# Key projection of the fourth head pair in an attention schedule: round 3 in place of round 5, and the last residual load behind round 5's transfers

## The chip, the core and the metric

The kernel runs on one core of a Trainium2 chip. A core has five engines that follow their own instruction lists and meet at semaphores: TensorE (PE, with its weight loads as PEld), VectorE (DVE), ScalarE (ACT), GpSimd (POOL) and SyncE (SP), which here issues all DMA transfers. The metric is the device time of one execution in microseconds.

## What is computed

Eight batches of 512 x 512 go through a gated cross attention and then through a gated mixture-of-experts self attention. The change touches the second part only:

```python
def _L0_ffn_ref(x, Wq, Wk, Ws, Wd, Wv, Wo):
    q = (x @ Wq).reshape(b, t, h, dh).transpose(0, 2, 1, 3)
    k = (x @ Wk).reshape(b, t, h, dh).transpose(0, 2, 1, 3)
    gl_v = (x @ Ws).reshape(b, t, h, e)
    wv = _topk_mask(gl_v, SEL) * jax.nn.sigmoid(gl_v)
    xv = jnp.einsum('btd,edk->btek', x, Wv)
    v = jnp.einsum('bthe,btek->bhtk', wv, xv)
    scores = jnp.einsum('bhid,bhjd->bhij', q * scale, k)
    probs = jax.nn.softmax(scores, axis=-1)
    attn = jnp.einsum('bhij,bhjd->bihd', probs, v)
    mask_o = _topk_mask(x @ Wd, SEL)
    return jnp.einsum('bthe,bthk,ekd->btd', mask_o, attn, Wo)

x = x + jnp.tanh(g_ffn[0]) * _L0_ffn_ref(_layernorm(x, axis=-1), ...)
```

There are 8 heads of 64 (4 pairs), 5 experts, 2 of them selected, 512 tokens and a model width of 512 per batch.

## The kernel before

The first part of the program (up to about 488 us of the profile) is the cross attention, which is not touched. The second, `expert_attention`, treats a batch in rounds. A batch has 32 tiles of scores (8 heads by 4 row tiles of 128 x 512), and a round is four of them, one for each of four PSUM banks: rounds 0 to 7 make the scores, pair p of heads using rounds 2p and 2p+1. Everything else of the batch is a unit that hangs at a round and at one of five places in it: SCORES, BEFORE, TURNS, BEHIND, AFTER. The table `AT` (line 1216 on) says where: `turn_y` transposes the normalised input, `experts` makes the expert values and logits, `q` and `k` project the queries and keys of a pair, `values` multiplies probabilities and mixed values, `turn_o` transposes a pair's output, `turn_z` and `result` make the output projection. Within a place, units come in the order in which the table was filled, so queries come ahead of keys.

Consecutive batches overlap. The loop `Fori(0, B - 1)` runs rounds 5 to 12 of batch b, and at each of their places also rounds -3 to 4 of batch b+1 (`CUT = 5`). So round 5 is joined with -3, round 7 with -1, round 8 with 0, round 11 with 3 and round 12 with 4. Ahead of the loop stand rounds -3 to 4 of the first batch, under a table `FIRST_AT` made from `AT` with four exceptions; behind it stand round 5 of the last batch by the same table and then `last_rounds`, written out by hand.

A projection is twelve matmuls of 128 x 512 (line 2219; `wk` is the keys' weight, the queries' lies in `c_t`). Each value is kept as a rounded part and a remainder: ScalarE copies the rounded part out of PSUM (`part_hi`, line 1735, keys at 1761) and VectorE subtracts it for the low part (`part_lo`, line 1928, keys at 1942). The units share three PSUM banks in ring order (`RING = 3`, `bank_of`): a unit's matmuls wait until the unit three places ahead in `ORDER` has been read (`wait_bank`, line 2180).

On the other engines the same tables set the order. VectorE takes row maxima (line 1880), transposes blocks of probabilities (1886), and makes the products of pair outputs and coefficients (1900). ScalarE exponentiates (1701), copies transposed probabilities (1710), normalises the next input (1679, in round -3) and copies expert tiles (1751, 1754). Before the first copy of a batch's expert tiles it waits until GpSimd has mixed all four pairs of the batch before. GpSimd mixes the experts' values of a pair (`mix_values`, lines 1610 and 1616) and adds products (1628). In rounds 4, 6 and 7 (`ALL_BY_VECTOR`) VectorE transposes all tiles in blocks; in the others TensorE transposes half of them (line 2281) and the rest goes through VectorE and DMA.

SyncE moves the block-transposed probabilities into place (`move_blocks`, line 1533: four DMAs of 128 KB for each half), loads the next input, stores the four output tiles of a batch, waits until they have landed and loads the next residual into the buffer that they came from. The values of pair p wait for the moves of rounds 2p and 2p+1.

Of the kernel before, what the change touches and what calls it, by code (L numbers as in the profile page):

```python
# [1167 lines left out]
def expert_attention(nc, block, both, x1, g_ffn, wk, wo, out):  # L1168
# [3 lines left out]
    B, T, D = x1.shape  # L1172
# [32 lines left out]
    SCORES, BEFORE, TURNS, BEHIND, AFTER = range(5)  # L1205
# [10 lines left out]
    AT = {}  # L1216
# [4 lines left out]
        AT["result", t] = ((12, BEFORE), (12, BEFORE), (12, BEHIND), (12, BEHIND))[t]  # L1221
    for p in range(PAIRS):
        AT["q", p] = ((-1, BEFORE), (0, BEHIND), (2, BEFORE), (3, BEFORE))[p]
        AT["k", p] = ((-1, BEFORE), (1, BEFORE), (2, BEHIND), (5, BEFORE))[p]
        AT["values", p] = ((3, AFTER), (5, AFTER), (7, BEHIND), (9, BEHIND))[p]
        AT["turn_o", p] = ((5, BEFORE), (7, BEFORE), (9, BEFORE), (10, BEFORE))[p]
    for k in range(KZ):
# [44 lines left out]
    with ExitStack() as mem:  # L1272
# [130 lines left out]
        def of(dram, b):  # L1403
            return dram[bass.ds(b, 1)].rearrange("o p t d -> (o p) t d")
# [16 lines left out]
        def blocks(r, i):  # L1421

            if i:
                return probs_odd[r % 2].rearrange("p s t -> p (s t)").rearrange("p (j s a) -> p j s a", s=2, a=BLOCK)
            return probs_even[:, r % 2]
# [25 lines left out]
        def by_rows(place):  # L1451

            return pt[:, place].rearrange("p k t -> p (k t)").rearrange("p (r q k s a) -> p r q k s a", r=2, q=QUADS,
                                                                        k=NT, s=2)
# [4 lines left out]
        def passing(name, half, k):  # L1459
            return raw[name][own_rows(name, half, k), k, :]  # L1460
# [4 lines left out]
        def first_end(eng):  # L1465

            eng.wait_ge(both.feat_ps, B * NT)
            eng.wait_ge(both.x1_ready, B * NT)
# [20 lines left out]
        def heads_moved(r):  # L1489
            return range(2 if r in ALL_BY_VECTOR else 1)  # L1490

        def tiles_moved(r):

            return sum(2 * len(heads_moved(i)) for i in range(r))
# [25 lines left out]
        @block.sync  # L1520
        def _(sp):
            def load_x1(b):
                sp.dma_start(stage[:], of(x1_dram, b)).then_inc(x1_loaded, 16)

            def load_residual(b):
                sp.dma_start(x_res[:], of(x1_dram, b)).then_inc(xres_loaded, 16)

            def store(b):
                for t in range(NT):
                    sp.wait_ge(out_ready, NT + b * NT + t + 1)  # L1530
                    sp.dma_start(of(out_dram, b)[:, t, :], x_res[:, t, :]).then_inc(out_stored, 16)

            def move_blocks(b, r, first=False):

                p = r // 2
                for i in heads_moved(r):
                    sp.wait_ge(blocks_turned, b * tiles_moved(ROUNDS) + tiles_moved(r) + 2 * i + 2)
                    if first and p == 2 and i == 0:

                        sp.wait_ge(o_ps, p - 1)  # L1540
                    for q in range(QUADS):
                        sp.dma_start(by_rows((2 * p + i) % 4)[:, r % 2, q].rearrange("p k s a -> p (k s a)"),
                                     blocks(r, i)[q * BLOCK:(q + 1) * BLOCK].rearrange(
                                         "p (j k) s a -> p j (k s a)", j=QUADS)).then_inc(moved[r % 2], 16)

            def steady(b, more):
                for r in range(CUT, ROUNDS):
                    move_blocks(b, r)
                    if more and r == CUT + 1:

                        sp.wait_ge(yt_ps, b * NT + 2 * NT)
                        load_x1(b + 2)
                for r in range(CUT):
                    move_blocks(b + 1, r)
                store(b)

                sp.wait_ge(out_stored, (b + 1) * NT * 16)
                load_residual(b + 1)

            first_end(sp)  # L1560
            for k in range(LAST):
                sp.dma_start(passing("wo", 0, k), wo[k * P:(k + 1) * P, :]).then_inc(wo_loaded[k], 16)
            for place in (0, HALF):
                sp.dma_start(wo_raw[place:place + HALF, LAST, :], wo[LAST * P:NV, :]).then_inc(wo_loaded[LAST], 16)
            sp.dma_start(gate_raw[:], g_ffn.partition_broadcast(P)).then_inc(gate_loaded, 16)

            sp.wait_ge(both.x1_stored, B * NT * 16)
            sp.wait_ge(both.x1_stats_done, B * NT)
            load_residual(0)

            sp.wait_ge(yt_ps, NT)
            load_x1(1)
            for r in range(CUT):
                move_blocks(0, r, True)
            with sp.Fori(0, B - 2) as b:
                steady(b, True)
            steady(B - 2, False)
            move_blocks(B - 1, CUT)
            for t in range(NT - 1):
                sp.wait_ge(out_ready, NT + (B - 1) * NT + t + 1)  # L1580
                sp.dma_start(of(out_dram, B - 1)[:, t, :], x_res[:, t, :]).then_inc(out_stored, 16)
            for half, cols in enumerate(LAST_COLS):
                sp.wait_ge(out_ready, NT + B * NT + half)
                sp.dma_start(of(out_dram, B - 1)[:, NT - 1, cols], x_res[:, NT - 1, cols]).then_inc(out_stored, 16)
            sp.wait_ge(out_stored, (B * NT + 1) * 16)
# [832 lines left out]
def program(nc, x, ctx, ctx_t, g_xattn, g_ffn, w_sim, w_sim_cols, b_sim, w_qv, b_qv, wq, wk, w_vsd, wo, x1, out):  # L2418
    B, T, D = x.shape
    NT, ND = T // P, D // P  # L2420
    with ExitStack() as mem:
        def sb(name, shape, dt=F32):
            return mem.enter_context(nc.sbuf_tensor(name, shape, dt))

        def sem(name):
            return mem.enter_context(nc.semaphore(name))


        x1_norm, x1_stats = sb("x1_norm", [P, 2, B * NT]), sb("x1_stats", [P, NT, 6])
        sb("fill", [P, 8])  # L2430
        both = Both(
            x1_norm=x1_norm, x1_stats=x1_stats, ident=sb("ident", [P, P]),
            x_sb=sb("x_sb", [P, NT, D]), stage=sb("stage", [P, NT, D]), spare=sb("spare", [P, 2, ND, D]),
            tmp=sb("tmp", [P, ND, T]), c_t2=sb("c_t2", [P, 2, ND, T], F32R), c_2=sb("c_2", [P, 2, NT, D], F32R),
            es_t2=sb("es_t2", [P, 2, ND, T], F32R), feat_ps=sem("feat_ps"), hc_ready=sem("hc_ready"),
            et_lo=sem("et_lo"), xb_ready=sem("xb_ready"),
            x1_ready=sem("x1_ready"), x1_stored=sem("x1_stored"), x1_stats_done=sem("x1_stats_done"),
            wx_loaded=sem("wx_loaded"), wq_loaded=sem("wq_loaded"), wk_loaded=sem("wk_loaded"), wx_hi=sem("wx_hi"),
            wx_lo=sem("wx_lo"), wq_hi=sem("wq_hi"), wq_lo=sem("wq_lo"), y_act=sem("y_act"), yt_ps=sem("yt_ps"),
            yt_hi=sem("yt_hi"), yt_lo=sem("yt_lo"))  # L2440
        block = mem.enter_context(nc.Block())
        cross_attention(nc, block, both, x, ctx, ctx_t, g_xattn, w_sim, w_sim_cols, b_sim, w_qv, b_qv, x1, w_vsd, wq, wk)
        expert_attention(nc, block, both, x1, g_ffn, wk, wo, out)
# [43 lines left out]
```

## Time and profile before

| | |
|---|---|
| time, median of 3 runs | 1133.11 us (1133.0 to 1133.26) |
| the profiled execution | 1133.13 us, of it span 1131.2 us |
| busy in the span: PE | 1100.8 us (97%) |
| busy: PEld | 836.7 us (74%) |
| busy: DVE | 925.1 us (82%) |
| busy: ACT | 567.4 us (50%) |
| busy: POOL | 657.4 us (58%) |
| granted TensorE clock over the span | 0.998 |

Times in the profile are microseconds from the start of the span. The busy shares are averages over both parts of the program. A row of a timeline names the start, the duration, the engine, the line of the kernel, what is written and read, how many instructions were merged into it (x12), and in brackets how long the engine was idle before it and what ended that. The ends of matmuls are modelled, so the distance between two starts says more of TensorE than a duration does.

### The profile page before, as it was taken

How to read it: one execution, taken by the hardware profiler on the slowest of the kernel's cores; microseconds unless marked ns; L12 is line 12 of the kernel's file. 1: busy time of each engine (PE TensorE's matmuls, PEld its weight loads, DVE VectorE, ACT ScalarE, POOL GpSimd, SP SyncE). 2: the span in 40 equal slices, each digit the busy share in tenths (PEclk: the TensorE clock that was granted, in tenths of full speed). 3: DMA queues.
4: the chain of work that ended last, by engine and by line, in shares of the span. 5: the costliest groups of instructions: out<-in, count | busy, mean ns of one | idle time of the engine just before them, and what ended most of it. 6: DMA issues, size and time to landing. Idle time of an engine off the chain costs nothing.

```text
span 1131.2 us, 18705 instructions
## 1 busy us (share of the span) xinstructions
PE 1100.8 (97%) x5709; PEld 836.7 (74%) x5709; DVE 925.1 (82%) x1609; ACT 567.4 (50%) x1295; POOL 657.4 (58%) x476
## 2 busy tenths in 40 slices
PE   7999999999999999999899999999999999999988
PEld 6888888888888888886666666767667666767656
DVE  7988787878777785758798897898988988978986
ACT  7644444344434343446655555455556545555533
POOL 2645252524333342337949759579499498596794
PEclk9999999999999999999999999999999999999999
DMA  5441414141414132442423524524426335244241
GB/s 205 149 140 47 131 56 130 56 130 56 130 56 130 56 93 72 144 132 69 127 75 93 171 71 124 154 56 137 123 56 190 88 74 178 77 115 128 52 137 38
DMA packets 89277, 119.97 MB, mean 106 GB/s; under 512 B 9120, under 2 KB 52896, under 8 KB 89248
## 3 DMA queue, kind: packets, MB, share of 16 engines
q1 hardware_dynamic: 89248, 119.61, 35.5%
q8 instruction: 15, 0.25, 0.1%
q14 instruction: 14, 0.11, 0.0%
HBM read 58.76 MB, written 16.78 MB: 67 GB/s over the span
## 4 chain that ended last, share of the span: by engine, by line
PE 70%; POOL 13%; DVE 9%; issue 5%; ACT 2%; DMA 0%; POOLq 0%; DVEq 0%; ACTq 0%
PE ps_f L992 23%; PE ps_s L992 8%; PE ps_o L2297 7%; PE ps_h L992 7%; POOL spare L1610 7%; PE ps_r L2219 6%; POOL spare L1616 5%; PE ps_r L2252 5%; PE ps_s L2273 5%; PE ps_r L2228 4%; DVE nmax L1880 2%; DVE beaten L1969 1%; POOL z L1628 1%; PE ps_r L2210 1%; DVE z_tmp L1900 1%
## 5 line engine op out<-in xcount | busy, mean ns | idle before, releaser
L1610 POOL TENSOR_TENSOR spare<-xv,pick 128x512 f32<-128x512 f32 x160 | 184.9, 1156 | 35.2 <-DVE pick L1996 22.3
L1880 DVE TENSOR_REDUCE nmax<-ps_s 128x1 f32<-128x512 f32 x256 | 158.2, 679 | 48.4 <-PE ps_s L2273 47.4
L1616 POOL TENSOR_TENSOR spare<-spare 128x512 f32<-128x512 f32 x128 | 165.8, 1295 | 10.0
L1628 POOL TENSOR_TENSOR z<-z,z_tmp 128x1280 f32<-128x1280 f32 x35 | 102.7, 2933 | 117.2 <-DVE z_tmp L1900 114.8
L1701 ACT ACTIVATE tmp<-ps_s,nmax 128x512 f32<-128x512 f32 x124 | 86.1, 695 | 106.8 <-DVE nmax L1880 106.8
L2297 PE MATMUL ps_o<-pt,spare 128*64 128x512 f32 x496 | 114.8, 605 | 9.4 <-POOL spare L1616 5.1
L254 POOL TENSOR_TENSOR e_t<-e_t 128x512 fp32r<-128x512 f32 x28 | 35.4, 1298 | 135.4 <-ACT e_t L510 135.4
L2273 PE MATMUL ps_s<-k,q 64*128 64x512 f32 x768 | 106.4, 408 | 0.7 <-ACT pt L1710 0.7
L2273 PEld LDWEIGHTS ps_s<-k,q 64*128 64x128 f32 x768 | 67.3, 184 | 42.9 <-issue 29.8
L254 POOL TENSOR_TENSOR c<-stage,c 128x512 fp32r<-128x512 f32 x28 | 41.3, 1508 | 95.9 <-ACT c L250 95.8
L2219 PE MATMUL ps_r<-es_t,c_t 128*128 128x512 f32 x384 | 96.2, 399 | 0.0
L2219 PE MATMUL ps_r<-es_t,wk 128*128 128x512 f32 x384 | 95.1, 396 | 0.0
L992 PE MATMUL ps_s<-c_t,es_t 128*128 128x512 f32 x384 | 92.5, 393 | 2.6 <-DVE es_t L727 2.6
L992 PE MATMUL ps_f<-wec,e_t 128*128 128x512 f32 x384 | 92.1, 392 | 0.0
L992 PE MATMUL ps_f<-weh,eh_t 128*128 128x512 f32 x384 | 91.9, 391 | 0.0
L992 PE MATMUL ps_f<-wh,h_t 128*128 128x512 f32 x384 | 91.3, 389 | 0.5 <-DVE h_t L887 0.5
L992 PE MATMUL ps_h<-es_t,c 128*128 128x512 f32 x384 | 88.7, 390 | 0.2 <-DVE es_t L781 0.2
L2297 PEld LDWEIGHTS ps_o<-pt,spare 128*64 128x64 f32 x496 | 33.4, 138 | 70.8 <-issue 64.0
L992 PEld LDWEIGHTS ps_s<-c_t,es_t 128*128 128x128 f32 x384 | 71.1, 188 | 17.8 <-DVE es_t L727 3.1
L992 PEld LDWEIGHTS ps_f<-wh,h_t 128*128 128x128 f32 x384 | 72.0, 188 | 15.9 <-DVE h_t L887 0.9
L992 PEld LDWEIGHTS ps_h<-es_t,c 128*128 128x128 f32 x384 | 71.9, 188 | 15.1 <-DVE es_t L781 0.3
L1886 DVE STREAM_TRANSPOSE tmp<-tmp 128x1024 f32<-128x1024 f32 x62 | 76.6, 1236 | 7.6 <-ACT tmp L1701 7.6
(253 smaller groups left out, 2272.4 us busy)
## 6 DMA issues: line engine op xcount, KB each, us to landing
pt<-tmp SPq DMA_DIRECT2D x248, 128.0 KB, 2.6
stage<-in_x SPq DMA_DIRECT2D x32, 256.0 KB, 3.3
x_sb<-in_x SPq DMA_DIRECT2D x8, 1024.0 KB, 5.2
x_dram<-x_sb SPq DMA_DIRECT2D x32, 256.0 KB, 3.1
stage<-x_dram SPq DMA_DIRECT2D x8, 1024.0 KB, 5.5
x_sb<-x_dram SPq DMA_DIRECT2D x8, 1024.0 KB, 5.7
out_dram<-x_sb SPq DMA_DIRECT2D x31, 256.0 KB, 2.7
pt<-probs_odd SPq DMA_DIRECT2D x60, 128.0 KB, 2.7
```

Of the source, the lines that this page charges most:

```text
L254: return eng.tensor_tensor(pair[:, 1, k, :], operand[:, k, :], pair[:, 0, k, :].bitcast(F32), ALU.subtract)
L992: last = pe.matmul(out, left(l, k), right(r, k), start=start and n == 1, stop=stop and n == ND * len(PASSES))
L1610: pool.tensor_tensor(v_tmp[:] if e else acc, xv[:, :, e, :].unsqueeze(2).broadcast_to(shape), pick[:, e, :, 2 * p:2 * p + 2].unsqueeze(3). ...
L1616: pool.tensor_tensor(acc, acc, v_tmp[:], ALU.add).then_inc(v_steps, 1)
L1628: pool.tensor_tensor(zv, zv, z_tmp[:, h % 2], ALU.add).then_inc(z_pool, 1)
L1701: act.activation(out, scores, ACT.Exp, bias=nmax[:, n:n + 1], accum_out=den[:, h, t:t + 1]).then_inc(p_exp, 1)
L1880: dve.tensor_reduce(nmax[:, n:n + 1], ps_s[:, n % BANKS, :], AX_X, ALU.max, negate=True).then_inc(nmax_ready, 1)
L1886: dve.transpose(both_tiles, both_tiles).then_inc(blocks_turned, 2)
L2219: end = pe.matmul(ps, w2[:, l, k, n * P:(n + 1) * P], y_t2[:, r, k, :], start=m == 0, stop=m == len(every) - 1)
L2252: end = pe.matmul(ps, z_t2[:, zt(l, k), n * P:(n + 1) * P], wo2[:, r, k, :], start=m == 0, stop=m == len(every) - 1)
L2273: end = pe.matmul(ps_s[:, (n + a) % BANKS, :], q2[head_rows(a), p % 2, l, t * P:(t + 1) * P], k2[head_rows(a), p % 2, r, :], start=m == 0, ...
L2297: end = pe.matmul(ps_o[head_rows(a), :], v_acc[:, p, k, a, :], rows, start=k == 0, stop=k == NT - 1)
```

## The change

The fourth pair's keys (pairs are counted from 0, so k3) are projected in round 3, behind the same pair's queries, and no longer in round 5. `FIRST_AT` takes the entry over, so this holds for the first batch too. On SyncE, in the run-down of the loop, the wait for the stored output of the last batch but one and the load of the last batch's residual now stand behind the moves of round 5 of the last batch; in the other turns the order is as it was.

```diff
@@
-        AT["k", p] = ((-1, BEFORE), (1, BEFORE), (2, BEHIND), (5, BEFORE))[p]
+        AT["k", p] = ((-1, BEFORE), (1, BEFORE), (2, BEHIND), (3, BEFORE))[p]
@@
                 for r in range(CUT):
                     move_blocks(b + 1, r)
                 store(b)
+                if more:
+                    replace_result(b)
+
+            def replace_result(b):
 
                 sp.wait_ge(out_stored, (b + 1) * NT * 16)
                 load_residual(b + 1)
@@
             steady(B - 2, False)
+
             move_blocks(B - 1, CUT)
+            replace_result(B - 2)
```

The lines behind the edit move by 4 to 6: the projections' matmuls are at 2225 after the change, the scores' at 2279.

On TensorE, at the joined round 11 and 3, before the change: q3 (`c_t`), then two tiles of probabilities (2281), the z transposes (2242) and the values of pair 0 (2297).

```order
L2219 MATMUL ps_r<-es_t,c_t 128x512 x12
L2279 REGISTER_ALU
L2281 MATMUL ps_s<-ident,spare 128x128 x4
L2279 REGISTER_ALU
L2281 MATMUL ps_s<-ident,spare 128x128 x4
L2238 REGISTER_ALU
L2242 MATMUL ps_r<-ident,z 128x128 x12
```

The same place after the change:

```order
L2225 MATMUL ps_r<-es_t,c_t 128x512 x12
L2225 MATMUL ps_r<-es_t,wk 128x512 x12
L2285 REGISTER_ALU
L2287 MATMUL ps_s<-ident,spare 128x128 x4
L2285 REGISTER_ALU
L2287 MATMUL ps_s<-ident,spare 128x128 x4
L2244 REGISTER_ALU
L2248 MATMUL ps_r<-ident,z 128x128 x12
```

Twelve key matmuls (`wk`) now stand between the queries' and the transposes.

On TensorE, at the joined round 5 and -3 of the loop, before the change: turn_o of pair 0 (2234), k3 (2219), two tiles of probabilities and the first of the four turn_y (2210).

```order
L2234 MATMUL ps_r<-ident,spare 128x128 x4
L2178 REGISTER_ALU
L2213 REGISTER_ALU
L2219 MATMUL ps_r<-es_t,wk 128x512 x12
L2279 REGISTER_ALU
L2281 MATMUL ps_s<-ident,spare 128x128 x4
L2279 REGISTER_ALU
L2281 MATMUL ps_s<-ident,spare 128x128 x4
L2178 REGISTER_ALU
L2208 ISA
L2210 MATMUL ps_r<-ident,stage 128x128 x4
```

The same place after the change:

```order
L2240 MATMUL ps_r<-ident,spare 128x128 x4
L2285 REGISTER_ALU
L2287 MATMUL ps_s<-ident,spare 128x128 x4
L2285 REGISTER_ALU
L2287 MATMUL ps_s<-ident,spare 128x128 x4
L2184 REGISTER_ALU
L2214 ISA
L2216 MATMUL ps_r<-ident,stage 128x128 x4
```

Only transposes are left there between the scores and the values of pair 1.

On SyncE, behind the loop, before the change: the stores of the last batch but one, the residual and the moves of round 5 of the last batch.

```order
L1542 DMA pt<-probs_odd 128x1x256 x4
L1531 DMA out_dram<-x_sb 128x512 x4
L1526 DMA x_sb<-x_dram 128x4x512
L1542 DMA pt<-tmp 128x1x256 x4
L1581 DMA out_dram<-x_sb 128x512 x3
```

The same place after the change:

```order
L1542 DMA pt<-probs_odd 128x1x256 x4
L1531 DMA out_dram<-x_sb 128x512 x4
L1542 DMA pt<-tmp 128x1x256 x4
L1526 DMA x_sb<-x_dram 128x4x512
L1587 DMA out_dram<-x_sb 128x512 x3
```

The moves and the residual have changed places.

## Rows read from the trace of the kernel before

**Rows 1.** The page, part 4: the chain that ended last, share by engine.

```profile
PE 70%; POOL 13%; DVE 9%; issue 5%; ACT 2%; DMA 0%; POOLq 0%; DVEq 0%; ACTq 0%
```

**Rows 2.** TensorE's waits: waiting line, releaser, us in total, times, longest.

```profile
PE ps_o L2297 <- POOL spare L1616: 5.1, 7, 0.7
```

**Rows 3.** Timeline of TensorE, joined rounds 11 and 3: q3 to the values.

```profile
752.57 3.03 PE L2219 MATMUL ps_r<-es_t,c_t 128*128 128x512 f32 x12
755.43 0.60 PE L2281 MATMUL ps_s<-ident,spare 128*128 128x128 f32 x4
...
757.09 1.53 PE L2242 MATMUL ps_r<-ident,z 128*128 128x128 f32 x12 [0.24 <-DVE z L1911]
759.36 3.65 PE L2297 MATMUL ps_o<-pt,spare 128*64 128x512 f32 x16 [0.73 <-POOL spare L1616]
```

**Rows 4.** Timelines of TensorE and ScalarE at round 7.

```profile
713.76 1.66 PE L2273 MATMUL ps_s<-k,q 64*128 64x512 f32 x12
...
714.68 0.24 ACT L1751 ACTIVATE logits<-ps_r 128x80 f32<-128x80 f32 x1 [4.04 <-POOL spare L1616]
...
715.35 0.66 PE L2234 MATMUL ps_r<-ident,spare 128*128 128x128 f32 x4
```

**Rows 5.** Timeline of TensorE in round 5, one weight load (PEld) with its wait.

```profile
693.88 1.66 PE L2273 MATMUL ps_s<-k,q 64*128 64x512 f32 x12
...
695.88 3.01 PE L2219 MATMUL ps_r<-es_t,wk 128*128 128x512 f32 x12
698.73 1.03 PE L2281 MATMUL ps_s<-ident,spare 128*128 128x128 f32 x8
699.60 1.34 PE L2210 MATMUL ps_r<-ident,stage 128*128 128x128 f32 x8
...
700.28 0.42 PEld L2210 LDWEIGHTS ps_r<-ident,stage 128*128 128x128 f32 x4 [0.32 <-ACT stage L1679]
...
700.87 3.65 PE L2297 MATMUL ps_o<-pt,spare 128*64 128x512 f32 x16
```

**Rows 6.** Timeline of ScalarE in round 5: first exponential, second normalised tile.

```profile
695.69 0.69 ACT L1701 ACTIVATE tmp<-ps_s,nmax 128x512 f32<-128x512 f32 x1 [6.29 <-DVE nmax L1880]
...
699.39 0.80 ACT L1679 ACTIVATE stage<-stage,norm 128x512 f32<-128x512 f32 x1
```

**Rows 7.** Timeline of TensorE, round 7 of the loop's first turn.

```profile
559.11 0.63 PE L2234 MATMUL ps_r<-ident,spare 128*128 128x128 f32 x4 [2.28 <-ACT logits L1751]
```

**Rows 8.** Timeline of TensorE in the last batch.

```profile
1095.50 0.66 PE L2234 MATMUL ps_r<-ident,spare 128*128 128x128 f32 x4
1100.39 5.22 PE L2297 MATMUL ps_o<-pt,spare 128*64 128x512 f32 x16 [4.23 <-issue]
...
1109.83 1.95 PE L2324 MATMUL ps_o<-pt,spare 128*64 128x256 f32 x16
```

**Rows 9.** Timeline of VectorE in round 5 of the last batch.

```profile
1090.70 0.68 DVE L1942 TENSOR_TENSOR k<-ps_r,k 128x512 fp32r<-128x512 f32 x1
...
1091.48 1.23 DVE L1886 STREAM_TRANSPOSE tmp<-tmp 128x1024 f32<-128x1024 f32 x1
```

**Rows 10.** SyncE's moves of round 5; landing of L1542 from 1092, and 1060 to 1090.

```profile
1093.38 2.77 SPq L1542 DMA_DIRECT2D pt<-tmp  x4
...
DMA to landing us min/median/max: 4.6/5.1/5.5
...
DMA to landing us min/median/max: 2.5/2.6/2.9
```

**Rows 11.** Timeline of GpSimd: the first sum behind its mixing.

```profile
1107.45 2.94 POOL L1642 TENSOR_TENSOR z<-z,z_tmp 128x1280 f32<-128x1280 f32 x1
```

**Rows 12.** Stretches: us, busy by engine, then granted clock, DMA share, GB/s.

```profile
1100.40:1105.60 5.20, 5.20 (x17) 1.61 (x18) 2.25 (x1) 0.00 (x0) 4.96 (x4) 0.69 0.01 3
```

**Rows 13.** Timeline of TensorE at the start of the kernel.

```profile
4.43 3.84 PE L999 MATMUL ps_b<-ident 128*128 128x128 f32 x18 [4.43 <-DVE stats L663]
...
9.44 1.04 PE L999 MATMUL ps_b<-ident 128*128 128x128 f32 x8
```

## The prediction

> **What bounds the kernel now.** I read the chain that ended last first, then TensorE's waits, then the timeline of one turn of the attention loop on each engine, then the end of the program. The chain is mostly TensorE, with a share of GpSimd [rows 1]: TensorE works nearly without a gap, so what counts is where its few gaps lie and who ends them. The reader should find two places.
>
> The first is round 11 of batch b, which is also round 3 of batch b+1. The projection of q3 starts at 752.57, the values of pair 0 start at 759.36 [rows 3], 6.79 us later. What runs in between is 2.86 for q3 (752.57 to 755.43), 0.87 for eight transposes of probabilities (698.73 to 699.60 [rows 5]) and 1.31 for the twelve transposes of z at the same pace, 5.04 in all. So 1.75 us are gaps: 0.73 of idle that GpSimd's mixing of the values ends and 0.24 that z ends, the rest lying in the modelled ends of matmuls. The wait for GpSimd comes seven times, once in each turn [rows 2].
>
> The second is round 7. There turn_o of pair 1 starts at 715.35. TensorE was ready just then (the scores start at 713.76 and hold it for 1.59), and so was the bank: ScalarE copied the first expert tile from 714.68 on, once GpSimd had mixed the last pair of the batch before [rows 4]. Two cycles are thus equally long, TensorE's own work with its gaps and GpSimd's mixing with the way back over turn_o, the scores, VectorE's products and the sums. A turn takes 78.12 us by either: from 559.11 in the first turn [rows 7] to 715.35 two turns later. This says at once that the loop can't gain: less work on TensorE would meet GpSimd at round 7. It can lose, if TensorE's own cycle grows.
>
> **Moving k3 in the loop.** The twelve matmuls cost 2.85 (695.88 to 698.73 [rows 5]).
> Added in round 3: between q3 and the values of pair 0 TensorE now has 5.04 + 2.85 = 7.89 us of work where it has 6.79 with its gaps. All gaps are covered, GpSimd is ready at 759.3 and the values start at about 760.45: 1.10 us later. ScalarE gets k3's copy ahead of its probability copies, VectorE the low part ahead of its block transpose. The last z transpose now goes to the bank that k3 used. VectorE's low part takes 0.68 [rows 9] and ScalarE's copy about as much, so that bank is free some 1.4 behind the end of k3; TensorE asks for it behind eight transposes and two thirds of the z transposes, 0.87 + 0.88 = 1.75. I take 0 for it, and 0.3 a turn as its bound.
> Removed in round 5: here the question is what stands behind k3. After the scores (693.88) VectorE takes the row maxima, ScalarE exponentiates from 695.69, then normalises two tiles of the next input, the second from 699.39 on; TensorE's weight load for the second turn_y waits for exactly that tile (idle 0.32, ended by ScalarE) and begins at 700.28, and the values of pair 1 follow at 700.87 [rows 5, 6]. That chain of 6.99 us from the scores to the values holds no k3: its copy on ScalarE comes behind both tiles, and its low part on VectorE comes behind the maxima. TensorE today fills that stretch with k3 and is just in time. With k3 gone it idles up to 2.85 us in small pieces and starts the values 6.99 after the scores as before. I take 0 for the gain; the bounds are 0 and 2.85, and the row with the wait for ScalarE stands for 0.
> So TensorE's cycle grows by 1.10 - 0 and GpSimd's no longer ties. From turn_o of round 7 in the first turn to the same place in the last there are six full turns: 6 x 1.10 = 6.6 us.
>
> **Before the loop and in its first turn.** The table for the first batch takes the new place too, so 2.85 are added in its round 3. Its round 5 is the first of the loop, with the same chain, and gives nothing back. But in that turn TensorE waits 2.28 at turn_o for GpSimd, which mixes from the first pick without a stop and is not touched [rows 7]. Cover 2.28, so 2.85 - 2.28 = 0.57 at most, 0 at least if some of the later gaps absorb it. I take 0.3.
>
> **The last batch.** Its rounds 3 and 4 are in the last turn and come 1.10 late against turn_o of that turn, as above. Then two edits meet. TensorE's turn_o of pair 1 is issued at 1095.50 and the values of pair 2 start only at 1100.39, after 4.23 of idle that no engine ended [rows 8]: they wait for the transfers of round 5. These four were issued from 1093.38 on, right behind a residual load of 1 MB, and took 4.6 to 5.5 us to land, where those of the rounds before took 2.5 to 2.9 [rows 10]. Now they go ahead of it. The blocks that they carry are transposed at 1091.48, behind the low part of k3 (some 0.6 of VectorE's time) [rows 9]; without that and with 1.10 of delay they are ready 0.5 later. The issues then start near 1093.2, the last one near 1095.2, and it lands by 1098.1. The values of pair 2 start 2.3 earlier. TensorE's idle before them shrinks from 4.23 to some 1.6, and with it may go the low clock: the granted clock was 0.69 from 1100.40 to 1105.60 and those 16 matmuls took 5.22 [rows 8, 12], against 3.65 in the loop. That is 1.57 more, 3.9 in all.
> What is late next is GpSimd. The first half of the last pair's values starts at 1109.83 [rows 8], and the mixing that it reads ended as GpSimd's first sum started, at 1107.45 [rows 11]. GpSimd's times hang on the last turn's round 8 and not on k3. So the end of the kernel can follow the values by 1109.83 - 1107.45 = 2.4 us and no more; the sums behind it, on GpSimd too, give the same. I take -2.35, with bounds of -1.2 (the transfers land late) and -3.6 (one collision less between VectorE's sums and GpSimd's mixing).
> The residual itself is read some 25 us after its new issue: nothing.
>
> **The sum.** The profiled execution took 1133.13 with a span of 1131.2 (the median of the runs is 1133.11): 1133.13 + 0.3 + 6.6 - 2.35 = 1137.7 us, 0.40% slower.
>
> **A rule against the rows.** At the start of the kernel TensorE runs transposes alone: eighteen from 4.43 take 3.84, 0.21 each, and eight from 9.44 take 1.04, 0.13 each [rows 13]. So transposes alone brought the fast pace. The Trainium skill, page "TensorE: Matmul & The Clock Gate", section "Part 4: PE-mode transpose", says that transposes don't count as work for the clock. By that rule the emptied round 5, where only transposes are left between the scores and the values, would fall to the lower clock. By it the sum is that of the clock's rival below, 1149; by the first rows of this kernel it stays at 1137.7, and I go by the rows.
>
> **Rivals.**
> *The stretch in round 5 does shrink.* If what makes the second turn_y late is partly k3 (a queue, a port), the values of pair 1 come earlier. From 1.10 on, the loss of round 3 is paid back and GpSimd binds at turn_o again: a turn takes 78.12, and the sum is 1133.13 + 0.3 - 2.35 = 1131.1, with the end's bound 1129.8. Against it: the weight load's wait names ScalarE's tile [rows 5]. Chance 0.13, half of it beyond 0.2%.
> *Half of it.* Part of the gaps in round 3 survive beside k3, or some 0.5 comes back in round 5: 0.3 to 0.6 a turn, 1133 to 1135. Chance 0.16.
> *The clock falls in round 5.* Between scores and values TensorE would idle for most of 5.4 us, which the tail's row prices: 1.57 more for sixteen value matmuls, in seven turns 11 us, so 1149. For it: after 4.23 of idle the clock was low [rows 12]. Against it: after the 2.28 of idle in the first turn turn_o took 0.63, as the 0.66 elsewhere [rows 4, 7], the pieces of idle here are shorter than that, and transposes stand between them [rows 13]. Chance 0.05.
> *The added matmuls are not added.* Each batch still projects k3 once, so the work is the same; a reader might expect no change. This sum, 1133.1 less whatever the end gives, holds only where TensorE alone binds at both places; it doesn't [rows 4, 5]. It would end with the first rival and has its chance there.
>
> **How the numbers follow.** The forecast has 0.66, with 1135.8 to 1140 for itself: the end's bounds give +1.2 and -1.2, the bank of k3 up to +2, the first turn 0.3 each way. This kernel's runs can tell 0.2% (2.3 us) from no change, so the same is 1130.9 to 1135.4. Faster: half the first rival, 0.07. Same: the other half and most of the second, 0.20. Slower: forecast, clock and the rest, 0.73. The range of 1132.5 to 1140 leaves out the first rival and the clock, 0.18.
>
> **What would show it.** Starts of turn_o in round 7 lie 79.2 apart, not 78.12. No wait for GpSimd at the values of pair 0, but several short ones for ScalarE in round 5, with 6.99 us from scores to values. The idle before the last batch's values of pair 2 under 2 us, with their sixteen matmuls back at 3.6, and a new wait for GpSimd's mixing before the last pair's. The forecast is wrong if the values of pair 1 follow the scores by less than 6.9, or if turns stay at 78.1.

## The result and the profile of the kernel after

| | before | after |
|---|---|---|
| median | 1133.11 us (1133.0 to 1135.09, 5 runs) | 1140.74 us (1140.43 to 1143.86, 5 runs) |
| after : before | | 1.007, interval 1.0055 to 1.0085 |
| profiled execution, span | 1133.13 us, 1131.2 us | 1143.86 us, 1142.1 us |
| granted clock over the span | 0.998 | 0.991 (0.994 in the other four) |

The change makes the kernel 0.7% slower. The direction was forecast; the time, 1137.7, was not, and 1140.74 lies above the range. The profiled execution of after is its longest, so where a size is given below it is that of this execution, and the medians of the experiments stand beside it. The ratios here and below compare the runs of both kernels as a whole, so they are not exactly the ratios of the medians beside them.

The page's chain, by engine, of after. GpSimd, which had 13% before [rows 1], is no longer in it:

```profile
PE 90%; ACT 5%; DVE 3%; issue 2%; DMA 0%; ACTq 0%; DVEq 0%
```

TensorE's waits in after (line, releaser, us in total, times, longest):

```profile
PE ps_s L2287 <- ACT spare L1707: 14.8, 16, 2.0
...
PE ps_o L2303 <- issue: 2.0, 1, 2.0
PE ps_r L2216 <- ACT stage L1685: 1.7, 5, 0.4
```

The seven waits for GpSimd at the values [rows 2] are gone. In their place stand sixteen for ScalarE's exponentials, two in each of the eight rounds 5, which the keys have left.

**Round 3**, TensorE's timeline (start, duration, operation), to be held against [rows 3]:

```profile
758.15 3.02 PE L2225 MATMUL ps_r<-es_t,c_t 128*128 128x512 f32 x12
761.01 2.89 PE L2225 MATMUL ps_r<-es_t,wk 128*128 128x512 f32 x12
763.74 1.03 PE L2287 MATMUL ps_s<-ident,spare 128*128 128x128 f32 x8
764.61 1.47 PE L2248 MATMUL ps_r<-ident,z 128*128 128x128 f32 x12
766.02 3.65 PE L2303 MATMUL ps_o<-pt,spare 128*64 128x512 f32 x16
```

From the start of q3 to the start of the values it is now 7.87 us, 1.08 more than before, with no idle left.

**Round 5, a turn at full clock**, to be held against [rows 5]:

```profile
699.57 1.66 PE L2279 MATMUL ps_s<-k,q 64*128 64x512 f32 x12
701.16 0.66 PE L2240 MATMUL ps_r<-ident,spare 128*128 128x128 f32 x4
702.87 0.66 PE L2287 MATMUL ps_s<-ident,spare 128*128 128x128 f32 x4 [1.06 <-ACT spare L1707]
704.21 0.66 PE L2287 MATMUL ps_s<-ident,spare 128*128 128x128 f32 x4 [0.68 <-ACT spare L1707]
705.21 1.36 PE L2216 MATMUL ps_r<-ident,stage 128*128 128x128 f32 x8 [0.35 <-ACT stage L1685]
706.51 3.65 PE L2303 MATMUL ps_o<-pt,spare 128*64 128x512 f32 x16
```

The values follow the scores after 6.94 us, nearly as before (6.99). The 2.85 us of keys have become 2.09 us of idle in three pieces, all ended by ScalarE; the rest lies in ends that are modelled. Only 0.05 is given back.

**Round 5, one turn later:**

```profile
784.34 1.82 PE L2216 MATMUL ps_r<-ident,stage 128*128 128x128 f32 x8 [0.35 <-ACT stage L1685]
786.09 4.63 PE L2303 MATMUL ps_o<-pt,spare 128*64 128x512 f32 x16
```

The idle is the same, but turn_y takes 1.82 instead of 1.36 and the values 4.63 instead of 3.65. The stretches show why (us, busy by engine, granted clock, DMA share, GB/s):

```profile
702.00:706.00 4.00, 2.04 (x13) 1.33 (x14) 4.00 (x5) 3.91 (x12) 3.77 (x4) 1.00 0.92 257
781.00:786.00 5.00, 2.97 (x16) 1.99 (x16) 5.00 (x6) 4.91 (x14) 4.69 (x5) 0.87 0.92 289
786.00:791.00 5.00, 5.00 (x20) 1.69 (x20) 2.33 (x3) 2.32 (x4) 4.69 (x5) 0.79 0.52 161
1023.00:1028.00 5.00, 4.86 (x18) 2.19 (x20) 4.14 (x5) 4.08 (x8) 4.69 (x5) 0.66 0.66 188
```

The column behind the five engines is the granted clock. It went from 2.4 to 1.2 GHz for part of the stretch: the mean is 0.87 and 0.79 in this turn and 0.66 in the round 5 at 1023, but 1.00 at 702.

**The turns.** A turn is measured from turn_o of round 7 to the next one. Here is one in which the clock fell:

```profile
720.97 0.66 PE L2240 MATMUL ps_r<-ident,spare 128*128 128x128 f32 x4
...
801.54 0.65 PE L2240 MATMUL ps_r<-ident,spare 128*128 128x128 f32 x4
```

turn_o of round 7 starts at 561.94, 641.88, 720.97, 801.54, 880.65, 959.75 and 1040.39. The six distances are 79.94, 79.09, 80.57, 79.11, 79.10 and 80.64, where before had six of 78.10 to 78.15, 78.12 in the mean. So there are two kinds of turn: three of about 79.10, and three that are 0.84, 1.47 and 1.54 longer, the ones in which the clock fell in round 5. It fell also in the round 5 ahead of the first of these starts, where the first piece of idle was 2.03 us long and the values took 5.29:

```profile
541.60 0.66 PE L2287 MATMUL ps_s<-ident,spare 128*128 128x128 f32 x4 [2.03 <-ACT spare L1707]
...
545.84 5.29 PE L2303 MATMUL ps_o<-pt,spare 128*64 128x512 f32 x16
```

**The last batch**, to be held against [rows 8]; first TensorE, then SyncE's issues, then GpSimd:

```profile
1108.40 0.66 PE L2240 MATMUL ps_r<-ident,spare 128*128 128x128 f32 x4
1111.05 5.35 PE L2303 MATMUL ps_o<-pt,spare 128*64 128x512 f32 x16 [1.99 <-issue]
...
1120.62 1.95 PE L2330 MATMUL ps_o<-pt,spare 128*64 128x256 f32 x16
```

```profile
1106.37 2.51 SPq L1542 DMA_DIRECT2D pt<-tmp  x4
1108.92 0.61 SPq L1526 DMA_DIRECT2D x_sb<-x_dram  x1
```

```profile
1119.86 2.91 POOL L1648 TENSOR_TENSOR z<-z,z_tmp 128x1280 f32<-128x1280 f32 x1
```

The moves now go ahead of the residual and land in 2.5 to 2.7 us (4.6 to 5.5 before [rows 10]). The idle before the values of pair 2 shrank from 4.23 to 1.99. But the sixteen matmuls behind it still took 5.35.

**The account** of the profiled executions: +2.83 up to the first turn_o, +9.72 in six turns (6 x 0.98 = 5.9 of it at full clock, 3.85 by the clock), -1.7 from the last turn_o to the end (101.7 instead of 103.4). That is 10.85, and the spans differ by 10.9.

### The profile page after: what moved, and what is told of

Read it like the earlier page. It is cut to its first block, busy times and chain, and to the rows that moved or that the text cites. A ratio compares the mean times of both kernels' runs of the same rounds, so it can differ in the third digit from the quotient of the medians.

```text
span 1142.1 us, 18712 instructions
## 1 busy us (share of the span) xinstructions
PE 1109.3 (97%) x5709; PEld 841.3 (74%) x5709; DVE 931.0 (82%) x1609; ACT 568.3 (50%) x1295; POOL 658.0 (58%) x476
## 4 chain that ended last, share of the span: by engine, by line
PE 90%; ACT 5%; DVE 3%; issue 2%; DMA 0%; ACTq 0%; DVEq 0%
PE ps_f L992 23%; PE ps_r L2225 15%; PE ps_o L2303 10%; PE ps_s L992 8%; PE ps_s L2279 8%; PE ps_h L992 7%; PE ps_r L2258 5%; PE ps_r L2234 4%; PE ps_s L2287 3%; PE ps_r L2216 1%; ACT tmp L1707 1%; PE ps_r L2240 1%; DVE nmax L1886 1%; ACT probs_odd L1707 1%; ACT spare L1707 1%
## 5 line engine op out<-in xcount | busy, mean ns | idle before, releaser
L2303 PE MATMUL ps_o<-pt,spare 128*64 128x512 f32 x496 | 118.9, 623 | 2.0 <-issue 2.0
```

The lines of the kernel that those rows point to most:

```text
L2303: end = pe.matmul(ps_o[head_rows(a), :], v_acc[:, p, k, a, :], rows, start=k == 0, stop=k == NT - 1)
```

## Experiments

Theory: three things add up. TensorE's turn grows by about 1 us since its cycle no longer ties with GpSimd's; the residual's new place gains 1 to 2 us; and TensorE's clock falls in some of the emptied rounds 5. Rivals: the excess lies in the residual's new place; it lies in something that the keys bring to round 3; the 2.85 us come back in round 5 and are lost elsewhere. Runs of one group were measured beside the same runs of the kernel before, whose median was 1135.02 in the first group (keys_only to fill_transposes), 1135.22 in the second (more_in_round_3 to tail_fill_only), 1133.75 in the third and 1135.13 for the last kernel. The ratios are to those runs. The kernel before has executions near 1133.3 and near 1135.1 (see the last experiment), and how many of each a group holds moves its ratios by about 0.1%. So 1.007 of the kernel after, whose five runs of before were nearly all of the short kind, and the ratios of the experiments are compared below by the kernels' own medians too.

### The two halves of the change

```diff
-        AT["k", p] = ((-1, BEFORE), (1, BEFORE), (2, BEHIND), (5, BEFORE))[p]
+        AT["k", p] = ((-1, BEFORE), (1, BEFORE), (2, BEHIND), (3, BEFORE))[p]
```

> Only the keys of pair 3 move to round 3; the last residual is loaded where it was. Theory (a turn grows by 1.0 to 1.1 us since round 3 gains more work than it had gaps and round 5 gives nothing back; in the emptied round 5 the clock falls in some turns, 0.9 to 1.5 us each; the end gains 1.7 by the residual): the loop as in the changed kernel, turns of 79.1 and some of 80 to 80.6, the end without its gain: 1142 to 1143.5. Rival (the two edits disturb each other, and the loss is partly the new order of transfers): 1140 or less.

Measured: 1144.77 us (1143.61 to 1145.89), ratio 1.0093 (1.0078 to 1.0109). Distances of turn_o: 80.50, 79.10, 79.10, 80.59, 79.12, 79.13.

The residual alone is the rest of the diff, with the keys in round 5.

> Only the last residual moves behind round 5's transfers; the keys stay in round 5. Theory: turns of 78.12 as before, the values of pair 2 in the last batch start 2 to 2.7 us earlier, the end is then bound by GpSimd's mixing: 1130.7 (1130.2 to 1131.5). Rival (the transfers are late for another reason, or the end is bound by GpSimd already): 1133.1.

Measured: 1133.17 us (1131.05 to 1134.5), ratio 0.9988 (0.9979 to 0.9997). TensorE and GpSimd in the last batch of its profiled execution:

```profile
1097.66 3.65 PE L2303 MATMUL ps_o<-pt,spare 128*64 128x512 f32 x16 [1.27 <-issue]
...
1107.73 1.95 PE L2330 MATMUL ps_o<-pt,spare 128*64 128x256 f32 x16 [2.12 <-issue]
```

```profile
1107.70 2.90 POOL L1648 TENSOR_TENSOR z<-z,z_tmp 128x1280 f32<-128x1280 f32 x1
```

The whole loss is the keys'. The residual's move gains 0.12%, and GpSimd stops the gain where the forecast said: the last pair's values start 0.03 behind GpSimd's first sum, that is, behind the end of its mixing, and 2.1 us earlier than before, not 3.9. Beside the keys the residual's move may be worth more than alone (1.0093 against 1.007, within the noise): in the profiled execution of keys_only TensorE waited 5.02 us before the values of pair 2, not 4.23, since it reached that place earlier against the transfers.

### Filling the emptied round 5

The kernel after, with unused work behind turn_o in round 5: ten matmuls, or 22 transposes, or two matmuls.

```diff
                 for what in units_at(n, place, table=FIRST_AT if first else AT):
                     shared(b, *what, first, last)
+                if n == CUT and place == BEFORE:
+                    work_again(b)
+
+            def work_again(b):
+                pe.wait_ge(out_ready, b * NT + NT)
+                for _ in range(10):
+                    pe.matmul(ps_r[:, bank_of(("turn_y", 1)), :], wk2[:, 0, 0, 0:P], wk2[:, 0, 0, :], start=True, stop=True)
```

> The changed kernel, with ten matmuls of 128x512 that nobody reads in round 5, in the place that the keys left, in a bank that is free. Theory: TensorE has 2.4 us to spare there, so they cost nothing; the values of pair 1 still start 6.9 behind the scores; the clock holds in all turns: seven rounds at 79.1 and 1137 to 1137.8. Rival A (round 5 gave time back): each turn grows, up to 2.4 x 7, 1145 and more. Rival B (the low clock has nothing to do with the emptied round): 1140.7.

Measured: 1137.22 us (1136.84 to 1138.62), ratio 1.0025 (1.0016 to 1.0034). All six distances are 79.09 to 79.14.

The same with transposes in place of the matmuls, against that kernel:

```diff
-                for _ in range(10):
-                    pe.matmul(...)
+                for _ in range(22):
+                    pe.transpose(ps_r[:, bank_of(("turn_y", 1)), 0:P], ident[:], ident[:])
```

> As the kernel with ten matmuls in the emptied round 5, but with twenty-two transposes of the identity (0.11 each, 2.4 us) in their place. If transposes hold the clock as matmuls do (what the start of the kernel before suggests): 1137 to 1137.8, no turn above 79.3. If transposes don't count as work for the clock (the Trainium skill, TensorE: Matmul & The Clock Gate, Part 4): as the changed kernel or worse, 1140 to 1144.

Measured: 1136.92 us (1136.7 to 1138.42), ratio 1.0023 (1.0014 to 1.0032), and a granted clock of 1.000 over the span in ten of eleven executions. One round 5, and the stretch around it:

```profile
698.09 2.56 PE L2324 MATMUL ps_r<-ident 128*128 128x128 f32 x22
700.49 1.04 PE L2287 MATMUL ps_s<-ident,spare 128*128 128x128 f32 x8
701.66 1.36 PE L2216 MATMUL ps_r<-ident,stage 128*128 128x128 f32 x8
702.96 3.65 PE L2303 MATMUL ps_o<-pt,spare 128*64 128x512 f32 x16
```

```profile
698.00:707.00 9.00, 8.81 (x61) 5.65 (x60) 7.72 (x9) 7.56 (x17) 8.37 (x9) 1.00 0.65 196
```

Adding work that nobody uses makes the changed kernel 3.5 and 3.8 us faster by the medians (from 1140.74 to 1137.22 and 1136.92, 0.31 and 0.33%; by the ratios 0.45 and 0.47%, for the reason given above). What it removes is the fall of the clock in round 5, and nothing else: the turns stay at 79.1, which is the round 3 part. Where only transposes fill the stretch the clock holds just as well. (The kernel before already has such unused transposes at its start, line 999, and ahead of its last outputs, line 2390, but none in the loop.) The Trainium skill, page "TensorE: Matmul & The Clock Gate", section "Part 4: PE-mode transpose", says that transposes do not count as the array being busy in the same way. By that rule this run would have kept the slow turns; the measurement decides, and here the clock held with them.

With two matmuls only (`range(2)` in the first diff):

> The kernel after the change with 2 unused matmuls of 128x512 (instead of 10) in the emptied stretch of round 5, behind turn_o. With 10 matmuls or 22 transposes there the clock held and the ratio to the kernel before was 1.0025 and 1.0023. With k3 in its old place but 11 of its 12 matmuls left out, TensorE idled 0.83, 0.68 and 0.35 a turn and in its profiled execution the values of pair 1 took 3.65 in five turns of seven. Theory 'the amount of idle decides, and it is near the edge': two matmuls take some 0.5 us of the 2.09 of idle away, so most turns hold the clock: ratio 1.0023 to 1.0035, 1137.2 to 1139, distances of turn_o in round 7 of 79.10 in five or six of six. Rival 'the whole stretch has to be filled': three turns of six at about 80.5 as in the kernel after, ratio 1.006 to 1.009.

Measured: 1141.09 us (1140.06 to 1142.34), ratio 1.0059 (1.0043 to 1.0076). Distances 79.12, 79.13, 80.58, 79.14, 79.14, 80.64. Idle in a turn is 0.60, 0.68 and 0.35, and the clock still fell in two of six turns and before the first:

```profile
780.17 0.66 PE L2287 MATMUL ps_s<-ident,spare 128*128 128x128 f32 x4 [0.60 <-ACT spare L1707]
781.51 0.66 PE L2287 MATMUL ps_s<-ident,spare 128*128 128x128 f32 x4 [0.68 <-ACT spare L1707]
782.51 1.83 PE L2216 MATMUL ps_r<-ident,stage 128*128 128x128 f32 x8 [0.35 <-ACT stage L1685]
784.27 4.66 PE L2303 MATMUL ps_o<-pt,spare 128*64 128x512 f32 x16
```

So the expectation that 0.5 us less idle is enough was wrong; the ratio is at the rival's edge, and the median is that of the kernel after (1140.74). The two slow turns are three apart (782 and 1021), as in keys_only (its first and fourth distance) and in after (784 and 1023, beside the one at 624). What sets that stays open.

### More work in round 3, less work in round 5

Before, with twelve unused matmuls added in round 3 and k3 left in round 5:

```diff
+                if n == 3 and place == BEFORE:
+                    work_again(b)
+
+            def work_again(b):
+                wait_read(b, ("q", 2))
+                for _ in range(12):
+                    pe.matmul(ps_r[:, bank_of(("turn_z", 0)), :], wk2[:, 0, 0, 0:P], wk2[:, 0, 0, :], start=True, stop=True)
```

> The kernel before, with k3 still in round 5, and twelve matmuls of 128x512 that nobody reads in round 3, where the change puts k3. Theory (round 3 covers 1.75 us of gaps and pays the rest; GpSimd no longer binds): turns of 79.1 to 79.2, round 5 as before, the clock high in all turns: seven turns, the first with its 2.3 us of cover, 6 to 7.5 us over the kernel before on the same chip, about as the changed kernel with a filled round 5 plus what the residual gives (1138.5 to 1140.5 where the kernel before takes 1133.1). Rival (the growth comes from the copies of k3 on ScalarE and VectorE or from the shifted banks, and not from TensorE's matmuls): 1133 to 1135.

Measured: 1141.8 us (1141.24 to 1142.04), ratio 1.0061 (1.0047 to 1.0075). turn_o starts at 559.25 and, six turns on, at 1034.26: 79.17 a turn, none slow.

```profile
559.25 0.63 PE L2234 MATMUL ps_r<-ident,spare 128*128 128x128 f32 x4 [0.84 <-ACT logits L1751]
...
1034.26 0.66 PE L2234 MATMUL ps_r<-ident,spare 128*128 128x128 f32 x4
```

Before, with eleven of the twelve matmuls of k3 left out, so that 11 x 0.24 x 8, some 21 us, of TensorE's work are missing:

```diff
                     every = [(k, l, r) for k in range(ND) for l, r in PASSES]
+                    if (name, n) == ("k", 3):
+                        every = every[:1]
```

> The kernel before, with eleven of the twelve matmuls of k3 left out in round 5 (the last pair's keys are wrong), its copies kept: 21 us of TensorE's work gone. Theory (the stretch from the scores to the values of pair 1 is bound by VectorE and ScalarE, and the clock falls in some turns once it is empty): values 6.9 to 7.0 behind the scores, turns of 78.1 and some up to 79.7, 1133 to 1139, not one faster than the kernel before. Rival (round 5 gives time back where TensorE has less to do): turns still 78.1 by GpSimd, but the values of pair 1 come 1 to 2.8 earlier and TensorE waits for GpSimd at turn_o of round 7.

Measured: 1135.26 us (1133.25 to 1136.92), ratio 1.0004 (0.9995 to 1.0013). One of its rounds 5:

```profile
693.96 1.66 PE L2275 MATMUL ps_s<-k,q 64*128 64x512 f32 x12
...
695.97 0.47 PE L2221 MATMUL ps_r<-es_t,wk 128*128 128x512 f32 x1
697.27 0.66 PE L2283 MATMUL ps_s<-ident,spare 128*128 128x128 f32 x4 [0.83 <-ACT spare L1701]
...
700.96 3.65 PE L2299 MATMUL ps_o<-pt,spare 128*64 128x512 f32 x16
```

These two are the forecast's mechanism with the keys' data taken out of it. Work added in round 3 costs 0.98 to 1.05 us a turn; 2.6 us a turn taken out of round 5 gain nothing, since the values stay 7.00 us behind the scores. keys_only less more_in_round_3 is 0.0093 - 0.0061 = 0.0032, 3.6 us (3.0 by the medians): the price of the emptied round. The two slow turns of keys_only's profiled execution, 1.40 and 1.49 longer than the others, hold 2.9 of it. The clock fell in round 5 of keys_left_out in two of seven turns of the profiled execution; GpSimd's wait hid one, the other made its turn 0.8 longer. That its turns are bound by GpSimd as well is one more reason why it gains nothing; that the 7.00 stands is what shows the chain through ScalarE.

### The clock in the last batch

Transposes behind turn_o of pair 1, and behind turn_o of pair 2, in the last batch:

```diff
                 shared(b, "turn_o", 1, False, True)
+                for _ in range(12):
+                    pe.transpose(ps_r[:, bank_of(("turn_o", LAST_PAIR)), 0:P], ident[:], ident[:])
...
                 shared(b, "turn_o", 2, False, True)
+                for _ in range(16):
+                    pe.transpose(ps_r[:, bank_of(("turn_o", LAST_PAIR)), 0:P], ident[:], ident[:])
```

On the kernel before, 34 transposes in the first place, none in the second:

> The kernel before, with 34 transposes that nobody reads in the 4.2 us in which TensorE waits for the transfers of the last batch's round 5. Nothing is earlier there; only the clock can stay high. Theory: the values of pair 2 start at the same distance and take 3.65 in place of 5.2 to 5.3, and the whole 1.6 arrives at the end, since GpSimd allows 2.4: 1131.5 where the kernel before takes 1133.1. Rival (GpSimd binds the end): 1133.1.

Measured: 1133.69 us (1133.13 to 1135.4), ratio 0.9993 (0.9984 to 1.0002). The values behind the fill took 3.65 instead of 5.22, but in the profiled execution they started 6.05 behind turn_o, not 4.89, because the transfers landed later: the moves took 5.0 to 5.9 us to land, not 4.6 to 5.5. The expectation of 1.6 us was wrong. The slow clock there cost the kernel before little or nothing that this run can tell.

On residual_only, both fills (12 and 16):

> The kernel with only the residual moved, and transposes that nobody reads in the last batch: 12 ahead of the values of pair 2 and 16 ahead of the last pair's (1.3 and 1.8 us, both within the idle there). Theory (the spread of the kernel with only the residual moved, 1131.0 to 1134.5, is the clock falling in these two gaps): all runs near its fastest, 1131.0 to 1131.6. Rival (the spread has another cause): the same spread as without them.

Measured: 1131.85 us (1131.35 to 1133.59), ratio 0.9976 (0.9967 to 0.9985).

On residual_only, the first fill only:

> The residual move alone with only the first fill of the last batch (12 transposes before the values of pair 2; none before the first half of the last pair's values). Keys are in round 5 as before. The move alone gave 0.9988, with both fills 0.9976. Theory 'GpSimd's mixing ends at about 1107.5 whatever TensorE does, and the fill only holds the clock': 0.9976 to 0.9985; TensorE waits 1 to 2 us for GpSimd before the first half of the last pair's values, which start within 0.1 of GpSimd's first sum. Rival 'the second fill is what matters, since the clock falls in the wait for GpSimd': 0.9988 as without fills.

Measured: 1132.36 us (1131.92 to 1134.38), ratio 0.9989 (0.9979 to 0.9998). TensorE at the place of the second fill, without it (residual_one_fill) and with it (residual_tail_fill):

```profile
1109.01 2.70 PE L2330 MATMUL ps_o<-pt,spare 128*64 128x256 f32 x16 [2.14 <-issue]
```

```profile
1109.22 1.95 PE L2330 MATMUL ps_o<-pt,spare 128*64 128x256 f32 x16 [0.39 <-issue]
```

The rival fits: the second gap matters, and the first fill alone changes nothing that can be measured. The ratios alone are too close to decide it (their intervals overlap), the rows do: from the start of these values to the end of the program it is 23.0 us without the second fill and 21.5 with it. None of the ten executions with one fill had a clock of 1.000 over the span, three of eleven without a fill and six of eleven with both. A fall in the first gap, some 1.6 us, would fit into the 2.12 us for which residual_only waits at the second (an estimate; none of these traces has one); what follows the second gap stands behind GpSimd and is on the path.

The kernel after with both kinds of fill (22 transposes in round 5, 12 in the last batch) is the change without any fall of the clock:

> The kernel after the change with 22 unused transposes in round 5 and 12 more between turn_o of pair 1 and the values of pair 2 in the last batch. It is the change without any fall of the clock. What is left is 6 turns of 0.98 or 1.0, some 0.3 at the start, and the gain of the last batch, -1.9 to -2.3 as in the run that moves the residual alone: 1133.1 + 0.3 + 5.9 - 2.2 = 1137.1 by the kernel's own time in a profiled execution, ratio 1.002 to 1.003. Theory: equal to the run with 22 transposes alone (1.0023) within 0.1%, since the clock of the tail held in 9 of its 11 executions already; the executions at a clock of 0.998 should become fewer. Rival 'the fill itself costs': the ratio is 1.003 or more.

Measured: 1136.93 us (1136.7 to 1138.02), ratio 1.0026 (1.0015 to 1.0038), span 1134.9 and clock 1.000 in the profiled execution, in which turn_o starts at 559.08 and 1033.85, 79.13 a turn. The change's own cost, without falls of the clock in its own executions, is 0.26% by the ratio; the spans differ by 3.7 us (0.33%).

### The first turn's wait

Most executions of the kernel before come in two groups, near 1133.3 and near 1135.1, at a clock of 0.998 and 0.997. The first turn has a wait of 2.28 us for GpSimd [rows 7]. The queries behind it, in the profiled execution of before and in that of residual_tail_fill, and the stretch in the latter:

```profile
559.57 2.96 PE L2219 MATMUL ps_r<-es_t,c_t 128*128 128x512 f32 x12
```

```profile
559.21 0.63 PE L2240 MATMUL ps_r<-ident,spare 128*128 128x128 f32 x4 [2.25 <-ACT logits L1757]
559.67 4.58 PE L2225 MATMUL ps_r<-es_t,c_t 128*128 128x512 f32 x12
```

```profile
559.70:564.00 4.30, 4.30 (x14) 3.43 (x13) 3.94 (x3) 2.99 (x10) 4.16 (x2) 0.61 0.73 246
```

turn_o took 0.63 in both, but the queries behind it 2.96 at full clock and 4.58 at 0.61. In the latter the clock was still high while turn_o ran, and low behind it:

```profile
559.20:560.60 1.40, 1.39 (x8) 1.23 (x9) 0.72 (x1) 1.40 (x7) 1.40 (x1) 1.00 0.80 109
560.70:564.00 3.30, 3.30 (x9) 2.62 (x8) 3.11 (x3) 1.99 (x6) 3.16 (x2) 0.50 0.75 291
```

To test it, residual_tail_fill with fifteen unused matmuls in round 3 of the first batch alone (`if first and n == 3 and place == BEFORE`), which use up that wait:

> The residual move with both fills of the last batch, and 15 unused matmuls of 128x512 in round 3 of the first batch only, ahead of the loop. In the loop's first turn TensorE waits 2.25 us for GpSimd at turn_o. In the profiled executions of the residual move with fills the queries behind that wait took 4.58 us at a granted clock of 0.61 and 0.60, in that of the kernel before 2.96 at 1.00. Twelve such matmuls there cut the wait to 0.84 in another run. Theory 'that wait lets the clock fall in about half of all executions, which costs 1.6 us': with the wait filled nearly all executions show a clock of 1.0 and take 1131.3 to 1132, ratio 0.9970 to 0.9977, and the spread of the kernel's runs is under 1 us. Rival 'the two groups of times of the kernel before come from somewhere else': half of the executions still take 1132.9 to 1133.6 at a clock of 0.998 and the ratio is 0.9976 to 0.9985.

Measured: 1131.77 us (1130.84 to 1132.49, 7 runs), ratio 0.9973 (0.9962 to 0.9984), and a clock of 1.000 in all seven. The wait is 0.18 and the queries are fast:

```profile
559.98 0.63 PE L2240 MATMUL ps_r<-ident,spare 128*128 128x128 f32 x4 [0.18 <-issue]
560.44 2.96 PE L2225 MATMUL ps_r<-es_t,c_t 128*128 128x512 f32 x12
```

So the group at 1135 is most likely a fall of the clock in the first turn; the trace of before is of the group at 1133, so for that kernel this is inferred. The spread of 1.65 us is more than the 1 us that I had expected. This kernel and residual_tail_fill are the best of the study; both beat before and after, and their intervals overlap.

## Why the prediction was wrong, step by step

- **Two cycles of equal length; the loop can't gain, and loses what TensorE's cycle grows: right.** More_in_round_3 shows it without moving anything.
- **Round 3 adds 1.10 a turn: right, a little large.** q3 to values grew by 1.08, the turn by 0.98: six turns cost 5.9 (6.04 in all_fills), not 6.6. The 1.75 of gaps also held 0.17 of idle that ScalarE ended, which the prediction put down to modelled ends. The bank of k3 cost nothing, as taken.
- **Round 5 gives back 0: right.** 6.94 in after, 7.00 in keys_left_out, ended by ScalarE. In the last batch, where no next input is normalised, scores to values is 5.15 instead of 5.82; those 0.67 come back there, and the sum had not seen it. It is also why TensorE's idle before the values of pair 2 is 1.99. The forecast said 1.6, but its own terms give 4.23 - 2.3 - 1.10 = 0.8; TensorE came only 0.35 later there, and the values 1.89 earlier.
- **The first turn costs 0.3: right in size.** At full clock turn_o starts at 559.08 with all fills and at 559.61 with ten matmuls, against 559.11: the term is 0 to 0.5. What after shows there, 2.83, has 0.49 that was there before round 3 began (the scores start at 523.53 instead of 523.04), and behind it the clock.
- **The last batch gains 2.35: right, and in after short by the clock.** In all_fills it is 2.35 from the last turn_o of the loop to the end (101.05 instead of 103.4). Residual_only starts the last pair's values 2.1 earlier and right at GpSimd's end. In after the gain is 1.7: the 1.57 of clock that the step said "may go" did not, and 5.35 for the sixteen matmuls brought TensorE to the last turn_o at 1120.04, 0.18 behind GpSimd's 1119.86. Residual_only gains 1.4 by the ratio and 1.9 by the medians, not 2.35, since in some executions the clock falls in the second gap.
- **The sum without the clock: +4.6 forecast, +3.7 in the spans of all_fills and before** (1134.9 and 1131.2). The two differ by the round 3 term (6.04 in all_fills, not 6.6) and the first turn (0, not 0.3).
- **"The clock falls in round 5", chance 0.05: this is the step that failed.** The clock's price was left out of the sum and of the range. The clock fell in part of the turns, and that is the whole miss: by the medians after less fill_transposes is 1140.74 - 1136.92 = 3.8 us (5.3 by the ratios), and fill_transposes itself is 0.8 under the forecast, which makes the 3.0 by which 1140.74 exceeds 1137.7. The rival had been priced as all or nothing, 1.57 in each of seven turns, and set aside; in the trace it was 0.84 to 1.54 in three of six turns, once ahead of them, and once in the tail. Two of its reasons did not hold. "After the 2.28 of idle in the first turn turn_o took 0.63": those are the four transposes right behind the wait, and the fall shows only in the queries after them, in some executions. The one profiled execution was one in which it did not fall there. "The pieces of idle are shorter than that": pieces of 1.06, 0.68 and 0.35 next to one another were enough, and 0.60, 0.68 and 0.35 too. The third reason, that transposes between them bring the clock [rows 13], is right as far as it goes (fill_transposes), but twenty of them in 5.4 us were not always enough. Half of the rival's 11 us in the range, for a clock that falls in half of the turns, would have taken it to 1143.
- **Rivals that fell:** the stretch in round 5 did not shrink, and no half of it came back.

## What to carry to other kernels

Work that only fills a wait is not free to move, even if both its old and its new place seem to have room: where it came from, the idle pieces it leaves can drop TensorE's clock, and what is behind them is then paid at 1.2 GHz. Price such a stretch in part, so many turns of so many, and put half of that price in the range, rather than all or nothing. Where a wait can't be shortened, a few unused transposes in it can be worth more than moving real work: here 22 a turn took 3.8 us (0.33%) off the changed kernel.

## What the runs showed of the hardware

- The granted clock fell after waits of 1.99 us (after) and 2.14 us (residual_one_fill), and in stretches where no single idle piece was longer than 0.68 us (two_matmuls). The same code kept it in other turns and other executions: the first turn's 2.25 us wait cost 1.6 us in residual_tail_fill and in residual_one_fill and nothing in residual_only. A single trace can't show that a wait is harmless.
- A fall need not show in the first instructions behind a wait: turn_o took 0.63 both times, the twelve matmuls behind it 2.96 or 4.58.
- Transposes hold the clock as matmuls do: 22 of them and ten matmuls of 128x512 took 2.56 and 2.54 us and gave 1.0023 and 1.0025.
- Four moves of 128 KB issued right behind a load of 1 MB took 4.6 to 5.9 us to land (before, tail_fill_only); issued ahead of it they took 2.5 to 2.7 us (after).
